# Attention scores from three float32r products, two heads side by side in the rows of the array

## What is computed

```python
xn = layernorm(x)
q, k, v = xn @ wq + bq, xn @ wk + bk, xn @ wv + bv   # 16 query heads, 2 key/value heads, 16 wide
q, k = rope(q) * 16 ** -0.5, rope(k)
scores = einsum('bqhd,bkhd->bhqk', q, k) * 16 ** -0.5
attn = einsum('bhqk,bkhd->bqhd', softmax(scores), v) @ wo + bo
hidden = fwht(silu(xn @ W1.T) * (xn @ W3.T))         # Hadamard transform over 1024
out = x + attn + hidden @ W2.T
```

## Time and profile before

| | |
|---|---|
| three runs | 1271.63, 1272.07, 1274.56 us; median 1272.07 |
| span of the profiled execution | 1273.1 us |
| the profiled execution beside the median | 1.0 us above it, within the three runs |
| first stage, up to the start of the down products of the last block | 375.3 us |
| first maxima matmul | 393.3 us |
| TensorE, VectorE, ScalarE, GpSimd busy | 1154.2, 882.7, 678.3, 159.5 us |

### The profile page before, as it was taken

One profiled execution on the slowest core, in us unless ns is written; L12 is line 12 of the kernel. 1 busy time (PEld: TensorE's weight loads), 2 busy tenths in 40 slices (PEclk: granted clock), 3 DMA queues, 4 the chain that ended last, 5 costly groups with the idle time before them and its releaser, 6 DMA issues.

```text
span 1273.1 us, 19955 instructions
## 1 busy us (share of the span) xinstructions
PE 1154.2 (91%) x6144; PEld 539.3 (42%) x6144; DVE 882.7 (69%) x1097; ACT 678.3 (53%) x1245; POOL 159.5 (13%) x251
## 2 busy tenths in 40 slices
PE   4798898899897899999999899899999989989984
PEld 3588788778882132232223223223223323323211
DVE  5856755775556987787868678678777867867500
ACT  2312321332230077767757667676776766767782
POOL 5503312330320000000000000000000001000000
PEclk9899999999896599999989899899999989989997
DMA  6011101101127105033024222422403403422211
GB/s 167 12 44 54 54 0 54 54 14 40 37 57 105 26 11 76 22 62 77 15 58 60 34 46 45 71 38 48 72 14 72 70 15 75 77 38 46 69 26 46
DMA packets 60684, 63.54 MB, mean 50 GB/s; under 512 B 20688, under 2 KB 40144, under 8 KB 60624
## 3 DMA queue, kind: packets, MB, share of 16 engines
q1 hardware_dynamic: 55760, 61.06, 23.7%
q10 hardware_dynamic: 4864, 1.84, 0.7%
HBM read 44.11 MB, written 13.89 MB: 46 GB/s over the span
## 4 chain that ended last, share of the span: by engine, by line
PE 71%; DVE 10%; DMA 7%; issue 5%; SPq 4%; ACT 2%; ACTq 1%; POOL 0%; POOLq 0%; DVEq 0%
PE ps L911 20%; PE ps L1051 17%; PE ps L1038 16%; PE ps L1006 15%; DMA dens<-osum 5%; DVE negmax L860 4%; PE ps L1016 2%; DVE xn L708 2%; ACT work L681 2%; SPq L392 1%; SPq L423 1%; SPq L396 1%; DMA k<-qk_parts 1%; PE ps L922 1%; PE ps L963 1%
## 5 line engine op out<-in xcount | busy, mean ns | idle before, releaser
L681 ACT ACTIVATE work<-ps 128x512 f32<-128x512 f32 x1024 | 561.9, 599 | 299.1 <-PE ps L1038 284.5
L860 DVE TENSOR_REDUCE negmax<-ps 128x1 f32<-128x1024 f32 x512 | 603.5, 1218 | 129.4 <-PE ps L1006 126.1
L1006 PE MATMUL ps<-k,w2h 96*128 96x512 bf16 x1024 | 333.6, 410 | 35.3 <-DVE negmax L860 26.9
L1051 PE MATMUL ps<-work,v 128*32 128x512 f32 x2048 | 279.1, 618 | 0.2
L911 PE MATMUL ps<-xnt_p,w_p 128*128 128x512 f32 x768 | 190.9, 402 | 5.6 <-DVE work L758 5.6
L1038 PE MATMUL ps<-q,k 99*128 99x512 bf16 x512 | 178.1, 395 | 6.3 <-ACT work L681 6.3
L1038 PE MATMUL ps<-qkp,k 99*128 99x512 bf16 x512 | 172.2, 386 | 10.0 <-ACT work L681 10.0
L1006 PEld LDWEIGHTS ps<-k,w2h 96*128 96x128 bf16 x1024 | 93.1, 101 | 197.2 <-DVE negmax L860 94.3
L911 PEld LDWEIGHTS ps<-xnt_p,w_p 128*128 128x128 f32 x768 | 142.8, 190 | 38.7 <-DVE work L758 5.9
L633 ACT ACTIVATE work<-ps 128x512 f32<-128x512 f32 x64 | 38.4, 599 | 216.4 <-PE ps L911 143.1
L1038 PEld LDWEIGHTS ps<-q,k 99*128 99x128 bf16 x512 | 48.8, 99 | 174.9 <-ACT work L681 122.4
(11 more groups left out here) (63 smaller groups left out, 584.5 us busy)
## 6 DMA issues: line engine op xcount, KB each, us to landing
w2h<-qk_parts SPq DMA_DIRECT2D x96, 128.0 KB
qk_parts<-qkp SPq DMA_DIRECT2D x24, 384.0 KB, 3.2
qkp<-qk_parts SPq DMA_DIRECT2D x48, 128.0 KB
q<-qk_parts SPq DMA_DIRECT2D x48, 128.0 KB
x_in<-in_x SPq DMA_DIRECT2D x8, 512.0 KB, 4.1
x_in<-osum SPq DMA_DIRECT2D x128, 32.0 KB, 2.0
xn<-recip_rows SPq DMA_DIRECT2D x128, 32.0 KB, 1.8
k<-qk_parts SPq DMA_DIRECT2D x32, 96.0 KB
```

Source lines behind the costliest of these rows:

```text
L681: nc.scalar.activation(prob[j % 2][:, h, :], ps[:, 4 + u % 3, :], ACT.Exp, scale=SCALE).then_inc(exp_done, 1)
L860: nc.vector.tensor_reduce(negmax[a % 2][:, h, t:t + 1], two, AX.XY, ALU.max, negate=True).then_inc(ring_free, 1)
L1006: m = pe.matmul(two[:, e, :], q1[p][:, h, t * P:(t + 1) * P], k1[p][:, e * 512:(e + 1) * 512], start=True, stop=True)
L1051: m = pe.matmul(ps[VW * h:VW * (h + 1), 7, :], v2[p][:, kt, :], prob[s % 2][:, h, :], start=(kt == 0), stop=(kt == ST - 1))
```

## The change

q and k are cut in two float32r parts instead of three bf16. VectorE writes the second part itself, GpSimd no longer splits. A score is three products in 48 rows: q's parts (0, 0, 1) against k's (0, 1, 0). Two heads stand side by side, in rows 0 to 47 and 64 to 111; k is there twice. An `S1` entry is now two heads by 512 keys, so VectorE reduces it to two partial maxima and combines the partial ones of a quad at its end. The maxima are turned in float32 and placed as two float32r rows for each half (50 rows in the scores). A step has three places instead of five: a pair of scores, a pair of scores, the sums. `q1`, `q2` and `k1` lie in buffers of the first stage (`w1_p`, `w3_p`, `xnt_p`), so the first loads also wait for the last gate and up products.

```diff
-NPROD = 6
-QPART = [0, 0, 0, 1, 1, 2]
-KPART = [0, 1, 2, 0, 1, 0]
-SROWS = NPROD * HD
-MROWS = 3
+PARTS = 2
+QPART = (0, 0, 1)
+SROWS = len(QPART) * HD
+MROWS = 2
+ROWT = 2
+PAIRS = QUAD // ROWT
+GRP = P // ROWT
...
-GAPS = QUAD + 1
-SUMS_AT = 4
+GAPS = PAIRS + 1
+SUMS_AT = PAIRS
-L_SCORE, L_SUMS = 512, 2200
-L_FILL = {"S1": 1024, "MT": 200, "WO": 4100}
+L_SCORE, L_SUMS = 1500, 2400
+L_FILL = {"S1": 600, "MT": 200, "WO": 4100}
...
-    parts = nc.dram_tensor("qk_parts", [3, 3, P, TOK], BF16).ap()
+    parts = nc.dram_tensor("qk_parts", [PARTS, 3, P, TOK], F32).ap()
...
+        q1, q2 = w1_p, w3_p
+        k1 = [xnt_p[p][:, :, :].rearrange("p c t -> p (c t)") for p in range(2)]
+        k2 = [sb(f"k2_{p}", [P, S], F32R) for p in range(2)]
...
-                for r in range(NPROD):
-                    src = parts[QPART[r], ds(g, 1), P // 2 * p:P // 2 * (p + 1), ds(b * S, S)]
-                    sp.dma_start(dst_q[p][r * HD:(r + 1) * HD, :, :],
-                                 src.rearrange("a (h d) t -> d (a h) t", d=HD)).then_inc(done[p], 16)
-                for r0, r1 in ((0, 3), (3, 5), (5, 6)):
-                    src = parts[KPART[r0]:KPART[r1 - 1] + 1, NG, ds(g * HD, HD), ds(b * S, S)]
-                    sp.dma_start(dst_k[p][r0 * HD:r1 * HD, :], src).then_inc(done[p], 16)
+                for r in range(ROWT):
+                    for n, part in enumerate(QPART):
+                        to = GRP * r + HD * n
+                        src = parts[part, ds(g, 1), P // 2 * p:P // 2 * (p + 1), ds(b * S, S)]
+                        src = src.rearrange("a (h r d) t -> r d (a h) t", r=ROWT, d=HD)[r]
+                        sp.dma_start(dst_q[p][to:to + HD, :, :].bitcast(F32), src).then_inc(done[p], 16)
+                    for to, a, z in ((GRP * r, 0, 2), (GRP * r + 2 * HD, 0, 1)):
+                        src = parts[a:z, NG, ds(g * HD, HD), ds(b * S, S)]
+                        sp.dma_start(dst_k[p][to:to + (z - a) * HD, :].bitcast(F32), src).then_inc(done[p], 16)
...
+            sp.wait_ge(lin_done, HC * NBLK)
...
-                for c in range(MROWS):
+                for r in range(ROWT):
+                    for c in range(MROWS):
...
+            def tokens(i):
+                norm_scale(i + 1)
+                residual(i + 1)
...
-                    nc.vector.tensor_reduce(negmax[a % 2][:, h, t:t + 1], two, AX.XY, ALU.max,
+                        dve.wait_ge(m_comb, 2 * i + a - 1)
+                    nc.vector.tensor_reduce(negpart[a % 2][:, :, h, t, e], two, AX.X, ALU.max,
                                             negate=True).then_inc(ring_free, 1)
+                    if b == 2 * STEPS - 1:
+
+                        dve.wait_ge(ring_free, n + 1)
+                        nc.vector.tensor_reduce(negmax[a % 2][:, :],
+                                                negpart[a % 2][:, :, :, :, :].rearrange("p r h t e -> p (r h t) e"),
+                                                AX.X, ALU.min).then_inc(m_comb, 1)
...
-                    for e in range(2):
-                        m = pe.matmul(two[:, e, :], q1[p][:, h, t * P:(t + 1) * P], k1[p][:, e * 512:(e + 1) * 512],
-                                      start=True, stop=True)
+                    for r in range(ROWT):
+                        rows = slice(GRP * r, GRP * r + SROWS)
+                        m = pe.matmul(two[:, r, :], q1[p][rows, h, t * P:(t + 1) * P],
+                                      k1[p][rows, half * 512:(half + 1) * 512], start=True, stop=True)
...
+                for r in range(ROWT):
+                    u = QUAD * j + ROWT * h + r
+                    before = u - 3 if u >= 3 else {0: -2, 1: -1, 2: -3}[u]
+                    if not (first and before < 0):
+
+                        pe.wait_ge(exp_done, QUAD * ITSTEPS * i + before + 1)
+                    rows = slice(GRP * r, GRP * r + SROWS + MROWS)
+                    pe.matmul(ps[:, 4 + u % 3, :], k2[p][rows, kt * P:(kt + 1) * P],
+                              q2[p][rows, h, half * 512:(half + 1) * 512], start=True, stop=True).then_inc(s2_done, 1)
```

More of the change, by code:

```diff
@@ L218, in build @@
         work = sb("work", [P, 2 * QUAD * 512])
-        cuts = [RQK, RQK, RQK, QKP, QKP, QKP, QKP, BLK, BLK]
+        cuts = [RQK, RQK, RQK, QKP, QKP, BLK, BLK]
         at = [sum(cuts[:n]) for n in range(len(cuts) + 1)]
         biased, rcos, rsin, *tiles = [work[:, a:b] for a, b in zip(at, at[1:])]
-        roped, rest, sg = tiles[0:2], tiles[2:4], tiles[4:6]
-        qkp = sb("qkp", [P, 3, 3, BLK], BF16)
+        roped, sg = tiles[0:2], tiles[2:4]
+        qk_p = [sb(f"qk_p{n}", [P, 3, BLK], F32R) for n in range(PARTS)]
         hid_p = [sb(f"hid_p{n}", [P, HC, BLK], F32R) for n in range(2)]
@@ L368, in store_parts @@
             def store_parts(i):
-                sp.wait_ge(part3_done, BT * (i + 1))
-                for c in range(3):
+                sp.wait_ge(rest_done, BT * (i + 1))
+                for c in range(PARTS):
                     sp.dma_start(parts[c].rearrange("a p t -> p a t")[:, :, ds(i * BLK, BLK)],
-                                 qkp[:, c, :, :]).then_inc(parts_out, 16)
+                                 qk_p[c][:, :, :].bitcast(F32)).then_inc(parts_out, 16)
             sp.wait_ge(xn_done, 1)
@@ L509, in residual @@
                                         ALU.add).then_inc(ybase_done, 1)
-            def split(i, first, last):
-                for t in range(BT):
-                    if t == 3 and not last:
-                        norm_scale(i + 1)
-                    pool.wait_ge(rest_done, BT * i + t + 1)
-                    cols = slice(t * P, (t + 1) * P)
-                    r = rest[t % 2][:, :].rearrange("p (a n) -> p a n", a=3)
-                    nc.gpsimd.tensor_tensor(qkp[:, 1, :, cols], r, zeros[:, :].unsqueeze(2).broadcast_to([P, 3, P]), ALU.add).then_inc(part2_done, 1)
-                    pool.wait_ge(part2_done, BT * i + t + 1)
-                    nc.gpsimd.tensor_tensor(qkp[:, 2, :, cols], r, qkp[:, 1, :, cols],
-                                            ALU.subtract).then_inc(part3_done, 1)
-                if not last:
-                    residual(i + 1)
+            def tokens(i):
+                norm_scale(i + 1)
+                residual(i + 1)
             pool.wait_ge(consts_set, N_CONSTS)
@@ L1032, in scores @@
                     pe.wait_ge(in2[p], N_IN * (i + 1))
-                    pe.wait_ge(mrows_in[p], 16 * MROWS * (i + 1))
-                before = u - 3 if u >= 3 else {0: -2, 1: -1, 2: -3}[u]
-                if not (first and before < 0):
-                    pe.wait_ge(exp_done, QUAD * ITSTEPS * i + before + 1)
-                pe.matmul(ps[:, 4 + u % 3, :], k2[p][:, kt * P:(kt + 1) * P], q2[p][:, h, half * 512:(half + 1) * 512],
-                          start=True, stop=True).then_inc(s2_done, 1)
+                    pe.wait_ge(mrows_in[p], N_ROWS * (i + 1))
+                for r in range(ROWT):
+                    u = QUAD * j + ROWT * h + r
[5 more added lines that the diff above has]
+                              q2[p][rows, h, half * 512:(half + 1) * 512], start=True, stop=True).then_inc(s2_done, 1)
             def sums(i, first, s):
@@ L1059, in iteration @@
                     if k != SUMS_AT:
-                        scores(i, first, j, k if k < SUMS_AT else k - 1)
+                        scores(i, first, j, k)
                     elif j > 0:
```

109 lines of the change are left out of this document (35 added, 74 removed).

## The result

The changed kernel takes 1413.21 us, median of 4 runs (1406.12 to 1422.62), where the kernel before took 1271.85 us in the same comparison (1268.76 to 1274.56). The ratio is 1.1116, with a 95% interval of 1.1058 to 1.1173. The forecast was 1301 us with a range of 1230 to 1345: slower, as said, but 141 us slower instead of 29.

What follows compares the result with a forecast made beforehand. TensorE's stream was taken to bound a full step, a score-exponential-sums loop the last pass. Terms: 1273.1 + 29 (transfers) + 9 (start) - 9 (first stage) + 0.5 - 1 = 1302, so about 1301 us; range 1230 to 1345.

Steps and rivals of the forecast that it cites:

- The clock falls: Rival, chance 0.05: TensorE streams some 70% of an attention step and drops to half speed; about 1710 us if throughout.
- Step 2: Loads ahead of the reciprocal at step 20: `dens` lands 7.8 us later; net of faster steps +29 us over seven passes.
- Step 1: Full attention step: row halves overlap, TensorE's stream no longer bounds; 2.69 us a step, 0.15 less than before.
- The loop: Attention step: first score, exponential, fourth score waiting for that bank, sums, next first score; 2.40 us before the change.
- turns: Rival, chance 0.13: row halves in attention do not overlap, TensorE bounds again at 3.05 us a step; about 1370 us.
- Step 4: First stage: GpSimd's splits go and normalisations shorten, partly offset by the residual add; 1.3 us a block, -9 us.
- The blocking: First stage: the residual add, moved ahead, blocks VectorE's two-input subtraction for up to 1.8 us.
- Step 3: Start of attention: first k and q loads take 24 us instead of 14.8 at the crowded rate; +9 us.
- Step 5: Small items: GpSimd's maxima split goes, VectorE gains a reduction and subtractions, +0.5 us in the lead; last pass -1.
- The loads get no longer: Rival, chance 0.20: at the step 20 reciprocal `dens` lands as early as before; 1231 us.
- Neither decides: Rival within the forecast's own range: the residual add blocks nothing and a step is 2.60 us; 1274 us, as before.

Runs made afterwards that it cites:

- 9: Changed kernel with score products contracted over all 64 rows of a half instead of 48 and 50, the added rows holding first-stage leftovers; 1325.42 us.
- 15: Changed kernel, products still in pairs, with SP's queue re-ordered and all 64 rows of a half in use; 1244.00 us.
- 5: Kernel before, with SP moving the sums' results ahead of the wait that the next iteration's second loads stand behind; 1235.04 us.
- experiment 2: Changed kernel, with SP moving the sums' results ahead of the wait that the next iteration's second loads stand behind; 1303.62 us.
- Experiment 1: Changed kernel with each 16-row block of k loaded by itself, so that no load steps over parts; 1357.25 us.
- 4: Changed kernel with one head's score product in each place of the step instead of a pair; 1338.27 us.
- 8: Kernel before with both score products contracted over the first 48 rows only, half of the terms left out; 1598.25 us.
- 12: Changed kernel with SP's queue re-ordered, products one at a time, all 64 rows of a half in use, zeros on the keys' side of added rows; 1203.49 us.
- 7: Changed kernel with each pair of maxima products issued twice into the same banks; 1399.26 us.
- 13: Changed kernel with SP's queue re-ordered and products one at a time, each score operand read as bf16; 1177.93 us.
- 10: Kernel before with both score products contracted over the first 64 rows only, a third of the terms left out; 1580.85 us.
- 14: Kernel before with each score product over 32 rows, alternating between rows 0 to 31 and 64 to 95; 1402.53 us.
- 11: Changed kernel with SP's queue re-ordered, products one at a time, and all 64 rows of a half in use, added rows holding leftovers; 1203.37 us.
- 6: Changed kernel with SP's queue re-ordered and its score products one at a time; 1227.95 us.

## Why the prediction was off, point by point

The runs split the 141 us, in one order of the edits. Filling the rows (9) takes 88 off: 1413 to 1325. Removing the waits from that kernel takes 81 more (15): 1325 to 1244. The same removal takes 37 from the kernel before (5), 1272 to 1235. So the waits that the change added are worth 81 - 37 = 44, and what is left between 1244 and 1235 is 9, the rest of the change. 88 + 44 + 9 = 141. By the ratios of each comparison the three are 89, 42 and 11, and their intervals leave the first some 9 us either way, the second 7, the third 4. In the other order, the waits first, the rows count for 60 and the waits for 73 (110 - 37). That split is rougher, as the runs of experiment 2 lie 40 us apart, but it shows that some of the loss arises only where the longer waits and the thin rows meet.

- **The step that failed is the rival "The clock falls", given 0.05.** The argument against it took the last pass before, at full speed with gaps, as proof that a TensorE with gaps keeps its clock. That looks at when the clock falls. What the change altered is how soon it comes back: 4 to 7 us before, up to 81 after, for 88 us in all (60 if the waits are taken out first). The sum had the clock at nothing, on this reading of when it falls. The two are different questions. The rows that bore on the second were there, the slices at 6 and 5 in the lead, where TensorE works with gaps for some 50 us and gets no more; I read them as the price of idling. Nor did the rival's time (1710, half speed throughout) allow the case that came, half speed for a part. The Trainium skill, page "TensorE: Matmul & The Clock Gate", section "Part 1: The HAM clock gate", puts the ramp at under 1% of a typical kernel's span; here it is 6% (88 of 1413).
- **Step 2, the transfers**, was right in mechanism and nearly in size: waits of 10.9 to 11.7 us for the 12 forecast. Experiment 1 shows the k loads that step over parts to be 7.7 us of it. The term read +29 and measured +44, beside 46.9 us of longer waits in the traces. The +29 counted steps 0.15 us faster, 25 x 7 x 0.15 = 26, which did not come; without them it is 7 x 7.8 = 55. The 44 hold whatever the longer waits cost in clock as well.
- **Step 1, the full step**, was mis-sized: 2.91 us instead of 2.69, so +0.07 instead of -0.15. The loop was the right one and the halves overlap, which ends the rival "turns". Two of its parts were mis-sized. From the first score to its exponential it takes 0.60 us (731.51 to 732.11) where the earlier trace rows have 0.43: +0.17 for the 0.025 forecast. From the fourth score to the sums it takes 0.65 us for 0.32, the whole second pair in between: +0.33 for the 0.265 forecast. Neither score stands behind another product, and alone it has a weight load of 0.18 or 0.19 us, where the bf16 loads of the kernel before take 0.10, and a length of 0.49 for 0.39. What each of these adds was not measured apart. With products one at a time the step is 2.69 us (4).
- **Step 4, the first stage**: -9 forecast; the down products of the last block start at 361.72 instead of 375.29, so -13.6. The four normalisations came as said, 1.38 us together. TensorE's wait for them fell to 0.93 us from 3.24, further than the 2 us forecast. The blocking came too:

```profile
269.92 2.45 POOL L505 TENSOR_TENSOR y<-x_in,bo_sb 128x1024 f32 x1
270.12 2.79 DVE L719 TENSOR_TENSOR hid_p<-work,hid_p 128x512 fp32r<-128x512 f32 x1
...
276.86 1.38 DVE L665 TENSOR_SCALAR xn<-x_in,mv,rstd 128x256 f32<-128x256 f32 x4
...
278.38 1.09 PE L886 MATMUL ps<-ident,xn 128*128 128x128 f32 x8 [0.93 <-DVE xn L665]
```

  VectorE's subtraction takes 2.79 us beside GpSimd's addition; alone it takes 0.69 (274.25).
- **Step 3, the start**: +9 forecast, 5.2 measured. Loads go out at 362.09 and the first maxima product runs at 383.60, 21.5 us; before it was 16.3.

```profile
383.60 1.22 PE L970 MATMUL ps<-xnt_p,w_p 48*128 48x512 f32 x4 [10.26 <-DMA xnt_p<-qk_parts]
```

- **Step 5** was not measured apart. Of the 9 us that are left over, the slower step makes 16 (0.07 x 224 steps in seven passes), the start 5.2, the first stage -13.6: 8.
- **The other rivals.** "The loads get no longer" fell with the wait of 11.05 us. "Neither decides" fell with the step, 2.91 us and not 2.60, and with the blocking. The halves do not take turns.

**What is shown of the clock, and what is open.** Shown: the time to full speed depends on the rows in use (8 against the kernel before, 9 against the change), though the added rows need not add to the product (12). A long wait is not what makes it long: stretches of 41 us and more follow waits of 3 to 4 us (1), and waits of 11 us end in short ones when the rows are full (9). More products in the step shorten it too (7), and so does issuing them one at a time instead of in pairs (4). It is not a matter of bf16 or float32r alone (13). All this fits one reading: at half speed the changed kernel gives the array less work per microsecond than the kernel before, though the records call TensorE busy in both. That reading also fits 10 and 14, where products of one half follow each other at a 5.39 us step, or have 32 rows. It was argued from these runs and not tried by itself, and how much work the chip wants stays open. So does why stretches in one execution of the changed kernel differ, 10 us and 81 after waits of the same length, and why the lead of experiment 2 stayed at half speed for 191 us in its profiled execution; its four runs lie 40 us apart, and the changed kernel's own lie 16 apart, where the kernels that return quickly lie 2 to 6 apart (5, 11, 12, 15).

**The version to keep** is that of experiment 12: the change, its products one at a time, SP's queue re-ordered, and the idle rows of each half filled with zeros. It takes 1203 us, by its ratio 5.5% less than the kernel before and 2.6% less than that kernel with its queue mended (1235).

## What to carry to other kernels

When a change makes TensorE's products smaller, ask not only whether its clock will fall but how the kernel gets it back after a wait that it already has. Three products for six looked like half of the work; by the reading above, it was the work that had brought the clock back. More rows in the contraction cost no time at full speed (2.91 us a step with 48 rows and with 64). They gave 88 us with leftovers in them (9), and 24 us in the mended kernel, with leftovers (11) or zeros (12) alike.

A wait that stands in the trace at each turn is worth mending first: the re-ordered queue gave 37 us to the kernel before, 110 to the changed one and 81 to that with full rows, and without it the change could not be judged.

When a loop is closed by a product that waits, count its weight load and its full length, not its rate in a stream.

## What the hardware showed that was not expected

- TensorE at 1.2 GHz with its records nearly without a gap, for up to 86 us in a row again and again (8), and once for 277 us (269 of them busy). A busy row of PE is no sign that full speed is near.
- Zeros on the keys' side of 14 to 16 more rows took the 58 us stretch of the last pass away: 1203 against 1228 us (12 against 6), with products of the same length, 0.39 us.
- Two float32r products in different row halves take 0.39 us together, and the next instruction starts 0.23 us after they do; at half speed these are 0.63 and 0.42 us (1109.10 to 1109.52). The halves work at once in bf16 as well (14).
- A two-input VectorE subtraction takes 2.79 us instead of 0.69 beside a GpSimd addition of 2.45 us.
